# The last strip's two cut chunks used in place, a row group of the array each, and their places loaded early

## The reference

```python
e = concatenate([u, i])                 # from x, W_u, W_i, diag, par
h = adj @ (adj.T @ e)                   # layer 0
x1 = layernorm(x + layernorm(h)*gamma + beta + x)
deg = adj.sum(axis=0) + 1.0             # layer 1
dinv = where(deg > 0, rsqrt(deg), 0)
z = dinv[:, None] * (x1 @ W)
out = layernorm(x1 + relu(dinv[:, None] * (adj.T @ z + z) + b))
```

## Time and profile before

| what | value |
|---|---|
| median of 3 executions | 629.25 us (627.91 to 630.54) |
| the profiled execution | 625.81 us |
| its span, first to last instruction | 624.1 us |
| PE busy | 597.0 us (96%) |
| DVE, ACT, POOL busy | 336.3, 135.8, 108.4 us |
| mean clock granted to PE | 0.989 of full |
| data moved by DMA | 204.81 MB, mean 328 GB/s |

### The profile page before, as it was taken

One profiled execution on the slowest core, in us unless ns is written; L12 is line 12 of the kernel. 1 busy time (PEld: TensorE's weight loads), 2 busy tenths in 40 slices (PEclk: granted clock), 3 DMA queues, 4 the chain that ended last, 5 costly groups with the idle time before them and its releaser, 6 DMA issues.

```text
span 624.1 us, 10849 instructions
## 1 busy us (share of the span) xinstructions
PE 597.0 (96%) x4784; PEld 237.3 (38%) x4784; DVE 336.3 (54%) x426; ACT 135.8 (22%) x197; POOL 108.4 (17%) x126
## 2 busy tenths in 40 slices
PE   8979999999999999999999999999999999977795
PEld 6433333333333333333333335554443334422232
DVE  3787666877867677886666783545140002600026
ACT  2015060331506033150604217211100001000001
POOL 3007042150705223050502205100000000000000
PEclk8979999999999999999999999999999999999998
DMA  8997896969788695978869597599999999999993
GB/s 311 387 377 259 285 362 206 389 218 335 262 290 330 220 389 202 348 265 289 312 239 388 184 364 275 180 337 420 422 419 422 422 423 420 421 423 422 412 387 113
DMA packets 77399, 204.81 MB, mean 328 GB/s; under 512 B 4126, under 2 KB 6686, under 8 KB 68136
## 3 DMA queue, kind: packets, MB, share of 16 engines
q1 hardware_dynamic: 76288, 203.27, 86.2%
q10 hardware_dynamic: 1064, 0.84, 0.4%
HBM read 202.79 MB, written 1.31 MB: 327 GB/s over the span
## 4 chain that ended last, share of the span: by engine, by line
PE 82%; DMA 11%; DVE 5%; SPq 0%; issue 0%; POOL 0%; ACT 0%; DVEq 0%; POOLq 0%
PE psum L795 31%; PE psum L905 23%; PE psum L994 13%; DMA turned<-in_adj_dram 7%; PE psum L913 6%; DMA slot<-in_adj_dram 4%; DVE slot L625 3%; PE psum L835 2%; PE psum L789 2%; PE psum L766 1%; PE psum L1015 1%; PE psum L972 1%; PE psum L960 1%; PE psum L857 1%; PE psum L1013 1%; PE psum L875 1%
## 5 line engine op out<-in xcount | busy, mean ns | idle before, releaser
L625 DVE STREAM_TRANSPOSE slot<-slot 128x2048 f32<-128x2048 f32 x80 | 177.7, 2279 | 75.4 <-PE psum L795 75.4
L795 PE MATMUL psum<-slot,E 128*64 128x512 f32 x800 | 179.3, 596 | 1.0 <-DMA slot<-in_adj_dram 0.8
L905 PE MATMUL psum<-slot,T 32*64 32x512 f32 x2560 | 143.7, 595 | 0.5 <-DVE T L609 0.5
L392 POOL COPY turned<-last_slot 32x1024 f32<-32x1024 f32 x80 | 84.4, 1055 | 277.8 <-DVE last_slot L625 273.4
L994 PE MATMUL psum<-slot,E 128*64 128x512 f32 x480 | 105.7, 594 | 8.6 <-DMA slot<-in_adj_dram 8.6
L795 PEld LDWEIGHTS psum<-slot,E 128*64 128x64 f32 x800 | 54.6, 137 | 113.9 <-issue 110.8
L443 ACT ACTIVATE turned<-last_slot 32x1024 f32<-32x1024 f32 x80 | 84.3, 1054 | 40.6 <-DVE last_slot L625 38.9
L905 PEld LDWEIGHTS psum<-slot,T 32*64 32x64 f32 x2560 | 54.7, 133 | 86.7 <-issue 82.6
L736 DVE TENSOR_TENSOR T<-psum,dinv 128x256 f32<-128x256 f32 x10 | 4.2, 424 | 140.8 <-PE psum L1015 140.2
L434 ACT ACTIVATE T<-T 32x256 f32<-32x256 f32 x60 | 24.8, 414 | 217.3 <-DVE T L609 216.0
L994 PEld LDWEIGHTS psum<-slot,E 128*64 128x64 f32 x480 | 35.0, 137 | 76.4 <-issue 76.2
(11 more groups left out here) (105 smaller groups left out, 268.1 us busy)
## 6 DMA issues: line engine op xcount, KB each, us to landing
slot<-in_adj_dram SPq DMA_DIRECT2D x152, 1024.0 KB, 14.2
last_slot<-in_adj_dram SPq DMA_DIRECT2D x30, 1024.0 KB, 7.5
turned<-in_adj_dram SPq DMA_DIRECT2D x9, 1024.0 KB, 16.2
X<-in_x_dram SPq DMA_DIRECT2D x5, 256.0 KB, 4.6
turned<-in_adj_dram SPq DMA_DIRECT2D x2, 512.0 KB, 12.1
out_dram<-T ACTq DMA_DIRECT2D x6, 128.0 KB, 7.2
out_dram<-T SPq DMA_DIRECT2D x4, 128.0 KB, 1.7
beta_b<-in_L_gnn_ln_beta_dram SPq DMA_DIRECT2D x1, 32.0 KB, 11.6
```

The source lines that it names most:

```text
L392: nc.gpsimd.tensor_copy(turned[c * Q32:(c + 1) * Q32, a].rearrange("p h k j r -> p (h k j) r"), last_blocks[a * Q32:(a + 1) * Q32, :, c, : ...
L625: v.transpose(parts, parts).then_inc(chunk_cut, 1)
L795: return mm(acc[half[b % 2], :], E[:, b, :], view[:, b % CB, :], start=(b < 2), stop=(b >= NB - 2))
L905: last = mm(acc[half[h], a, :], T[step % 2][rows_a, jb, d, :], slot[step % 2][rows_a, h:NF:2, :, cols], start=step == 0 and jb == 0 and d ...
```

## The change

- The last strip's chunks 8 and 9 are no longer moved into `turned`. The new `h_end` uses them in `last_slot` as DVE cut them, with 32 matmuls for each `jb`, 128 in all, of 32 rows, 64 columns and 128 moving columns. It stands between `h_group(step, 2)` and `h_group(step, 3)` of the last step. The eight `h_last` matmuls of the last step are gone.
- `h_end` adds into the first 128 columns of banks 4 to 7. What the nine earlier strips left in the other 384 columns of bank 4 is first copied by ACT into `end_part`. DVE then puts group 4 of `h` together with one copy and one add (`end_ready`) into `between`. ACT's `copy_hT(4)` is gone.
- On ACT, `square_h(1)` goes ahead of the copy of groups 2 and 3, `root_h(1)` ahead of `copy_yT(0)`; on PE, `sum_h(1)` stands ahead of `turn_y(0)`.
- The two places in `turned` become place numbers 16 and 17 and are loaded as soon as step 8's last products are done (`turned_used`); the two of `last_slot` become 18 and 19 and are loaded after `h_end` (`end_done`). Both stand ahead of load 0; `LATE` is gone.

```diff
-            if q == NF:
+            if q == NF + 1:
                 return last_slot[:, s], last_loaded[s], NJ
@@ sync
-            sp.wait_ge(moved_act, NJ * len(ACT_MOVES))
-            sp.wait_ge(moved_pool, NJ * len(POOL_MOVES))
+            sp.wait_ge(turned_used, NJ - 1)
             for s in range(RES):
                 load_first(s, NF)
+            sp.wait_ge(end_done, 1)
+            for s in range(RES):
+                load_first(s, NF + 1)
             for n in range(LOADS):
-                if n == LATE:
-                    sp.wait_ge(h_done, 2)
-                    for s in range(RES):
-                        load_first(s, NQ - 1)
@@ gpsimd
-            for step in range(NJ):
+            for step in range(NJ - 1):
@@ scalar
-                move(step)
+                if step < NJ - 1:
+                    move(step)
+            act.wait_ge(turned_used, NJ - 1)
+            nc.scalar.activation(end_part, bank[4][:, P:4 * P].rearrange("p (a n) -> p a n", n=P), ACT.Copy)\
+              .then_inc(end_moved, 1)
             root_h(0)
+            square_h(1)
             copy_hT(2, 2)
-            square_h(1)
+            root_h(1)
             copy_yT(0)
             root_y(0)
-            root_h(1)
@@ vector
+            dve.wait_ge(end_done, 1)
+            dve.wait_ge(end_moved, 1)
+            v.tensor_copy(end_hT[:, 0], h_sums(NG - 1, 1)[:, 0]).then_inc(end_ready, 1)
+            v.tensor_tensor(end_hT[:, 1:4], h_sums(NG - 1, 1)[:, 1:4],
+                            end_part.rearrange("p a (k r) -> p a k r", r=Q32), ALU.add).then_inc(end_ready, 1)
@@ tensor
+            def h_end(jb):
+                for d in range(4):
+                    for a in range(4):
+                        c = (a + d) % 4
+                        cols = slice(jb * P + c * Q32, jb * P + (c + 1) * Q32)
+                        rows_a = slice(a * Q32, (a + 1) * Q32)
+                        for h in range(2):
+                            last = mm(end_acc[half[h], a, :], T[(NJ - 1) % 2][rows_a, jb, d, :],
+                                      last_slot[rows_a, h, :, cols], start=a > 0 and jb == 0 and d == 0, stop=False,
+                                      skip_group_check=True)
+                return last
@@ h_step
                 h_group(step, 2)
+                if final:
+                    pe.wait_ge(chunk_cut, NJ * NQ)
+                    pe.wait_ge(dinv_sum, 1)
+                    for jb in range(JB):
+                        last = h_end(jb)
+                    last.then_inc(end_done, 1)
                 h_group(step, 3).then_inc(slots_used if not final else h_done, 1)
@@ the passage
-            last_products([0])
             sum_h(0)
             turn_h(0)
             turn_h(1)
+            sum_h(1)
             turn_y(0)
-            last_products([1])
             sum_y(0)
             project_y(0)
-            sum_h(1)
             first_round(1)
...
-            last_products([2, 3]).then_inc(h_done, 1)
             turn_h(2)
```

More of the change, by code:

```diff
@@ L91, in build @@
         xT = [turn[1][:, :], sb("xT", [P, JW])[:, :]]
-        hT = [turn[0][:, :], turn[1][:, :], between[:, 0:JW], between[:, JW:2 * JW], turn[0][:, :]]
-        hh = [after[:, 0:JW], after[:, 0:JW], between[:, 2 * JW:3 * JW], between[:, 3 * JW:4 * JW], after[:, 0:JW]]
+        hT = [turn[0][:, :], turn[1][:, :], between[:, 0:JW], between[:, JW:2 * JW], between[:, 2 * JW:3 * JW]]
+        hh = [after[:, 0:JW], after[:, 0:JW], between[:, 3 * JW:4 * JW], after[:, 0:JW], between[:, 3 * JW:4 * JW]]
         yy = after[:, JW:2 * JW]
@@ L129, in build @@
         acc = psum[:, 0:4, :]
+        end_acc = psum[:, 4:8, 0:P]
+        end_part = between[:, 3 * JW:3 * JW + 3 * P].rearrange("p (a n) -> p a n", n=P)
         t_acc = bank[5]
@@ L186, in build @@
         spread_dve = sem("spread_dve")
+        end_moved = sem("end_moved")
+        end_done = sem("end_done")
+        end_ready = sem("end_ready")
         h_done = sem("h_done")
@@ L219, in h_sums @@
                 return acc[:, :, g * P:(g + n) * P].rearrange("p a (k r) -> p a k r", r=Q32)
-            return bank[4].rearrange("p (a k r) -> p a k r", k=CB, r=Q32)
+            return end_acc.rearrange("p a (k r) -> p a k r", r=Q32)
         def copies(g):
-            return g + 1 if g < 3 else g
+            return min(g + 1, 3)
         def feat(v, n=GB):
@@ L453, in copy_hT @@
             def copy_hT(g, n=1):
-                act.wait_ge(h_done, 1 if g < NG - 1 else 2)
-                if g == NG - 1:
-                    act.wait_ge(h_turned, 1)
+                act.wait_ge(h_done, 1)
                 to = hT[g] if n == 1 else between[:, 0:n * JW]
@@ L466, in square_h @@
                 else:
-                    act.wait_ge(hT_ready, copies(g))
-                    if g in (1, NG - 1):
-                        act.wait_ge(h_summed, 1 if g == 1 else 2)
+                    if g < NG - 1:
+                        act.wait_ge(hT_ready, copies(g))
+                    if g in (2, NG - 1):
+                        act.wait_ge(end_ready, 2)
+                    if g != 2:
+                        act.wait_ge(h_summed, g if g == 1 else g - 1)
                     nc.scalar.activation(hh[g], hT[g], ACT.Square).then_inc(hh_ready, 1)
@@ L513, in _ @@
             root_y(3)
-            copy_hT(4)
             square_h(4)
@@ L670, in _ @@
             dve.wait_ge(residual_centred, NG)
+            end_hT = hT[NG - 1].rearrange("p (k a r) -> p a k r", k=CB, r=Q32)
+            dve.wait_ge(end_done, 1)
[3 more added lines that the diff above has]
+                            end_part.rearrange("p a (k r) -> p a k r", r=Q32), ALU.add).then_inc(end_ready, 1)
             def norm_h(g):
@@ L849, in turn_h @@
             def turn_h(g):
-                pe.wait_ge(hT_ready, copies(g))
+                if g < NG - 1:
+                    pe.wait_ge(hT_ready, copies(g))
                 if g == 0:
@@ L870, in sum_h @@
                 if g == 0:
+                    pe.wait_ge(end_ready, 2)
                     pe.wait_ge(pairs_ready, 2)
@@ L924, in h_step @@
                 if final:
+                    pe.wait_ge(end_moved, 1)
                     turn_degrees()
```

1 line of the change is left out of this document (removed).

## The result

The changed kernel took 635.33 us in the median of 5 (634.78 to 637.35), the kernel before 629.25 us; the ratio is 1.0112, with a 95% interval of 1.0081 to 1.0143. The change makes the kernel slower. The time lies well above the forecast of 629.8 us and inside the forecast's range, 627.0 to 637.0 us.

A forecast was written before the change was run, and what follows sets the result against it. The end of the second pass's load stream was taken as the bound. PE's shift at sweep 15, H + 0.2 - 1.72 = 3.5 us, less the 3.0 us margin, gave 0.5 us later: 629.25 to 629.8 us, range 627.0 to 637.0.

The forecast's parts named there:

- the case that I thought likeliest: `h_end` on PE runs near the array's pace, 3.5 to 7.5 us; time 628.2 to 632.3 us; chance 0.57.
- Rival B: Instruction supply on PE bounds `h_end`, 7.5 to 14 us; at 43 ns a record 635.8 us; chance 0.30.
- The length of `h_end`: Time H of the new matmuls on PE's path ahead of `h_done`: 5.0 us, range 3.5 to 14.0.
- C: Pieces of the array no longer overlap for short matmuls: 63 ns a record, 640.9 us; chance 0.03.
- What leaves PE: Last step's `h_last` matmuls go, 1.72 us gained on PE's path; matmuls beside waits and moved `sum_h(1)`: 0.2 us lost.
- The margin of 3.0 us at load 15: Load queue's backlog at load 15, 7.7 - 4.7 us: PE delay under 3.0 us up to there costs nothing.
- The costs beside other work: ACT's copy, DVE's group 4 copy and add, and the removed moves lie beside PE's work and cost nothing.
- (2): Sign: loads into `turned` go out at about 371 us; rate from 380 to 385 us near 388 GB/s.
- (5): Sign: no row with DVE's or ACT's work for group 4 on the chain.
- (1): Sign: new matmuls' length first to last, 4 to 7 us for the likeliest case, over 7.6 for Rival B.
- (3): Sign: first sweep begins at 400.9 us; load 15 goes out near 446.2 us, lands about 4.7 us later, queue empty.
- (4): Sign: the last load lands at about 610.9 us.

The follow-up runs named there:

- e1: The changed kernel, but the two loads into `turned` wait for `h_end` too; 633.65 us, ratio 1.0073 to the kernel before.
- e4: The changed kernel with three pairs of idle matmuls in PE's waits in the passage; 634.23 us, ratio 1.0080 to the kernel before.
- e3: The changed kernel with only the first quarter of the new matmuls (`jb` 0); 628.53 us, ratio 0.9991 to the kernel before.
- e2: The changed kernel with the new matmuls dealt out in 16s between those of `h_group`; 637.39 us, ratio 1.0110 to the kernel before.

## Why the prediction was right or wrong

The forecast was an end 0.5 us later; measured were 9.3 us in the profile and 6 to 8 us in the timed runs. The range held, and the sign of the middle value; the case that I thought likeliest did not. Rival B's 635.8 us lies next to the measured 635.33, but B came to it by 43 ns for every record, where the new ones took 15 and then 30 ns with a hole between, so that nearness is luck. That the range held is B's doing too.

**What bounds the kernel: right.** The end of the load stream sets the end; from load 15 to the last landing all kernels take 167 to 170 us, whatever was changed ahead of it. (The load that the prediction calls the last, landing at 610.4 us, is load 78; the halves of load 79 land later and end no wait. The difference between the kernels is not touched by this.)

**The length of `h_end`: mis-sized, H = 5.0 us against 8.5.** The bound from the array was good: 15 ns for a record at the start, 244 records in 3.9 us when nothing disturbs (e1), near the 4.0 us of the prediction's rounds. The step that failed is that I had looked for the supply's limit in the spacing of the instructions and not in where they come from. The hole adds 3.1 us, of which 2.5 are the change's own early loads (e1), and the lower clock behind it 1.3 us (3.07 against 1.74 us). Without the early loads `h_end` is 4.6 us long, near the 5.0; but PE then stops once more at the next 256 instructions, so that the last step still grows by 6.0 us. The early loads, which I had costed at nothing on PE, make it 8.6: 2.6 us more. Of the rivals, B had named the place, and a price near it (7.5 to 14 us), but another mechanism: a pace for every record, where the trace has a fast pace and a hole. C's price for pieces that don't overlap, 63 ns a record, was refuted at 15 ns, and with it the page's rule of 81 ns (the Trainium skill, "TensorE: Matmul & The Clock Gate", Back-to-back issue gap), for pieces of the array. The page gives that figure for a stream of pairs; that pieces stop overlapping, as C has it, it doesn't say.

**What leaves PE: right on the path, wrong beside it.** The 1.72 us of the two last `h_last` pairs were gained (load 0 to load 15 went from 45.1 to 43.4 us). The pairs in the gaps and `sum_h(1)` I priced as 0.1 gained and 0.3 lost, by what PE waits for. At the full clock the passage would have been 0.5 us shorter, since PE's waits (0.7 to 0.8 us) are shorter than the matmuls that filled them (1.0 us); the lower clock costs 2.6 us, and the measured price is the difference, 2.1 us (e4). The prediction had the waits, and didn't ask what an idle PE does to its clock.

**The margin of 3.0 us at load 15: wrong.** I had taken 4.7 us, the landing of a load that goes out alone, for the floor. In the changed kernel load 15 lands 6.6 us behind its issue, in e3 7.5 us, though the stream isn't full there. Loads 13, 14 and 15 go out 2.7 and 3.9 us apart, closer than a landing takes, so the load ahead of it is still under way. In the changed kernel:

```profile
slot<-in_adj_dram SPq DMA_DIRECT2D x1, 1024.0 KB, 6.6
```

The margin was thus 7.7 less 6.6 to 7.5, 0.2 to 1.1 us, and e3 shows no more than that: load 15 goes out 0.1 us later and lands 0.1 us earlier. With H and the passage as measured the prediction's sum would be 8.5 + 2.1 - 1.7 - 3.0 = 5.9 us; without the margin it is 8.9, and 9.3 were measured. The statement that a delay of PE of less than 3.0 us costs nothing no run bears out.

**The costs beside other work: right.** ACT's copy, DVE's copy and add, and the lost moves stand nowhere on the chain. **The signs**: (2) and (5) came as written, and (1) came as B. (3) and (4) failed: the first sweep began at 404.2 us, load 15 went out at 451.3 us and took 6.6 us, and the last landing was at 619.3 us. Two slips of the prediction change nothing: B and C together have a chance of 0.33, where it says 0.34 for slower, and the issue at 384.23 us follows the last of POOL's moves (384.15 us), not of ACT's.

## What to carry to other kernels

Short matmuls on pieces of the array can use up PE's instructions faster than they arrive, and dealing them out among longer ones doesn't help by itself (e2). Count PE's instructions: the stops came at fixed places, 256 instructions apart. Don't keep big loads in the queue while such matmuls run, since here the packets of instructions came late behind them. Before matmuls are taken out of a wait because they are hidden there, check whether they keep the clock up. A load moved from a full stretch to an idle one pays only if what releases the later loads is faster than the stream; compare the releases per microsecond with the stream's rate, and take the landing time of a load in its own company, not of one alone.

## What the runs showed of the hardware

Matmuls of 32 x 64 by 128 columns on eight pieces of the array go at 15 ns a record with their weight loads (142 in 2.16 us), where a full-array record of 128 columns takes 126 ns: an eighth of 126 ns is 15.8, so the eight pieces overlap fully, as long as instructions are at hand. PE's holes stood behind matmul record 3644, 3772 or 3900 in all seven kernels that have one, 256 instructions apart, as are the 16 KB packets of instructions, and ended 2.2 to 2.9 us behind the start of such a packet. 1 MB loads in the queue moved the packet by 2.4 to 2.8 us. After the hole of 3.1 us the granted clock stood at half for some 3 us of work; after one of 0.63 us it did not fall. Three waits of 0.7 to 0.8 us within 10 us were followed by half clock as well, and with matmuls in them the clock stayed full.
